# A cross-attention and FFN kernel: tiles of 128 queries, scores on row strips, fp32 products, and a written order for each engine

## What is computed

```python
q = (x @ Wq).reshape(b, n, 32, 8); k, v = split(ctx @ Wkv)       # x: layernormed
q, k = apply_axial_rope(q, pos), apply_axial_rope(k, pos)
w = softmax(einsum('bqhd,bkhd->bhqk', q, k) / sqrt(8))
x = x + einsum('bhqk,bkhd->bqhd', w, v).reshape(b, n, 256) @ Wout + bout
h = square(relu(ln(x) @ up_w))                                     # 256 -> 1024
y = h @ down_w + (ln(x) @ expert_weight) * top2(ln(x) @ gate_w).sum()
x = x + layernorm(y) * gamma + beta
```

## Time and profile before

| | us |
|---|---|
| median of 3 runs | 252.93 |
| lowest and highest | 249.64, 253.37 |
| span of the profiled execution | 250.5 |

### The profile page before, as it was taken

One profiled execution on the slowest core, in us unless ns is written; L12 is line 12 of the kernel. 1 busy time (PEld: TensorE's weight loads), 2 busy tenths in 40 slices (PEclk: granted clock), 3 DMA queues, 4 the chain that ended last, 5 costly groups with the idle time before them and its releaser, 6 DMA issues.

```text
span 250.5 us, 4919 instructions
## 1 busy us (share of the span) xinstructions
PE 221.1 (88%) x1754; PEld 175.5 (70%) x1754; DVE 167.7 (67%) x374; ACT 141.3 (56%) x284; POOL 105.3 (42%) x129
## 2 busy tenths in 40 slices
PE   2959768899999999999998999998889999778980
PEld 1847535677777787879786878877557886567980
DVE  6965899868886789684559974745998100572455
ACT  3256457597767675865647667564446967111520
POOL 7774566731238014474653136231324454332003
PEclk9995799999999999999999999999999999955896
DMA  7943141102101101010101110101000000000001
GB/s 199 357 94 84 47 107 45 28 20 62 48 24 29 42 3 48 0 48 0 47 0 43 46 47 0 46 3 44 0 27 21 5 0 3 0 0 22 3 21 42
DMA packets 12743, 10.68 MB, mean 43 GB/s; under 512 B 2992, under 2 KB 12336, under 8 KB 12720
## 3 DMA queue, kind: packets, MB, share of 16 engines
q1 hardware_dynamic: 11680, 10.37, 14.7%
q10 hardware_dynamic: 1040, 0.01, 0.2%
HBM read 5.13 MB, written 1.05 MB: 25 GB/s over the span
## 4 chain that ended last, share of the span: by engine, by line
PE 68%; DVE 18%; issue 6%; ACT 3%; POOL 2%; DMA 1%; POOLq 0%; DVEq 0%; ACTq 0%
PE ps_bg L956 18%; PE ps_bg L939 11%; PE ps_st L1037 11%; PE ps_o L1053 10%; PE ps_s L1021 9%; PE ps_dn L1109 9%; DVE mneg L837 7%; DVE stats L702 2%; DVE mnat L844 1%; PE ps_st L972 1%; DMA pos_sb<-in_fside_BxSx 1%; DVE mnat L845 1%; DVE by_token L710 1%; ACT kmask L612 1%; DVE rot_c L766 1%
## 5 line engine op out<-in xcount | busy, mean ns | idle before, releaser
L837 DVE TENSOR_REDUCE mneg<-ps_s 128x2 f32<-128x512 f32 x128 | 84.6, 684 | 36.4 <-PE ps_s L1021 35.7
L641 ACT ACTIVATE probs<-ps_st 128x512 f32<-128x512 f32 x128 | 73.3, 595 | 26.4 <-PE ps_st L1037 26.1
L1037 PE MATMUL ps_st<-qstack,kmask 128*128 128x256 f32 x256 | 57.3, 308 | 0.5 <-ACT probs L641 0.4
L1021 PE MATMUL ps_s<-kmask,qstack 128*128 128x512 f32 x128 | 54.4, 428 | 3.1 <-DVE mneg L837 1.9
L1037 PEld LDWEIGHTS ps_st<-qstack,kmask 128*128 128x128 f32 x256 | 39.9, 189 | 15.1 <-issue 9.5
L473 POOL TENSOR_SCALAR var_eps<-mv 128x1 f32<-128x1 f32 (+1 forms) x20 | 7.1, 353 | 75.0 <-DVE mv L705 74.9
L1053 PE MATMUL ps_o<-probs,vaug 128*32 128x256 f32 x512 | 34.3, 385 | 0.0
L1021 PEld LDWEIGHTS ps_s<-kmask,qstack 128*128 128x128 f32 x128 | 25.1, 197 | 7.2 <-DVE mneg L837 5.2
L956 PE MATMUL ps_bg<-x2nT,up 128*128 128x256 f32 x192 | 27.3, 296 | 1.0 <-ACT x2nT L573 1.0
L956 PEld LDWEIGHTS ps_bg<-x2nT,up 128*128 128x128 f32 x192 | 26.1, 202 | 2.0 <-ACT moe L672 1.4
L1109 PE MATMUL ps_dn<-down,inner 128*128 128x256 f32 x192 | 25.4, 283 | 0.2 <-DVE inner L341 0.2
(11 more groups left out here) (109 smaller groups left out, 311.5 us busy)
## 6 DMA issues: line engine op xcount, KB each, us to landing
kmask<-kstack SPq DMA_DIRECT2D x60, 64.0 KB, 2.1
x_sb<-in_x SPq DMA_DIRECT2D x4, 256.0 KB, 6.6
whole<-in_L_ffn_down_w SPq DMA_DIRECT2D x4, 256.0 KB, 5.4
qstack<-mT SPq DMA_DIRECT2D x64, 4.0 KB
result<-y_fin SPq DMA_DIRECT2D x8, 128.0 KB, 1.7
c_sb<-in_ctx SPq DMA_DIRECT2D x4, 128.0 KB, 2.4
oT<-in_L_ffn_up_w SPq DMA_DIRECT2D x1, 512.0 KB, 5.5
y_fin<-in_L_ffn_up_w SPq DMA_DIRECT2D x1, 512.0 KB, 7.4
```

Of the source, the lines that this page charges most:

```text
L641: act.activation(probs[n % 2][:, i, :, :], ps_st[k % NST][:].rearrange("p (t n) -> p t n", t=T), ACT.Exp, scale=SCALE).then_inc(st_free, 1)
L837: dve.tensor_reduce(mneg[m % 2][:, t, n % 2, 2 * half:2 * half + 2], ps_s[(4 * n + k) % NS][:].rearrange("p (i k) -> p i k", i=2), AX.X, A ...
L1021: pe.matmul(ps_s[(4 * n + k) % NS][:], qstack[b % 2][:, g, t * P:(t + 1) * P], kmask[:, g, 2 * half:2 * half + 2, :], start=True, stop=Tru ...
L1037: ins = pe.matmul(ps_st[k % NST][:, t * N:(t + 1) * N], kmask[:, g, i, t * P:(t + 1) * P], qstack[b % 2][:, g, :], start=True, stop=True)
```

## The change

The kernel is rewritten around another tiling; what is computed stays the same.

- Five written orders (`PE_ORDER`, `DVE_ORDER`, `ACT_ORDER`, `POOL_ORDER`, `SP_ORDER`) replace the one list with due times. An entry is a kind and its numbers.
- The tile is 128 queries (8 tiles `u`); a step `M` (32 of them) is one tile and one pair of head groups, 8 heads. FFN, output and expert products go by tile `u`.
- S and ST are matmuls on one row strip of 32 rows, so `kmask` and its DMAs go. An entry `B.k.n` of `PE_ORDER` is a burst: the two ST units number `k-1` on two strips and the two S units number `n-1` on the other two, interleaved.
- K and Q are computed transposed (weights as the loaded operand, their columns permuted by ScalarE at the start), so the 128 transposes of `nat` go. cos and sin are spread over rows and transposed once per batch (`TR`). Six DMAs for K and six for each part of Q (`shi`, `slo`) put the high and low parts into the rows of `kstack` and `qstack`.
- All products with weights are plain fp32, without split.
- The maxima are split on GpSimd (`mh`), most normalisations and squares are there too.
- PSUM: three banks for S, three for ST, two for all else, now with P·V and down. Four `probs` buffers. No `keep_warm`.

```diff
+PE_ORDER = """
+cT.0 V.0 TR.0 K.0 xT.0.0 cT.1 xT.0.1 Q.0.0 TR.1 TR.2 Q.0.1 xT.1.0 TR.3 K.1 V.1 cT.2 B.0.1 Q.1.0 B.0.2 xT.2.0
+B.0.3 K.2 MT.0 B.0.4 B.0.5 B.0.6 MT.1 B.1.7 Q.2.0 xT.3.0 B.2.8 MT.2 B.3.9 PV.0 B.4.10 MT.3 B.5.11 PV.1 MT.4
+B.6.12 B.7.13 PV.2 MT.5 B.8.14 B.9.15 PV.3 MT.6 B.10.16 o.0 B.11.17 PV.4 MT.7 B.12.18 aT.0 B.13.19 W.0 MT.8
...
+B.60.0 up0.3 B.61.0 E.3 x2T.5 up1.4 dna.2 dna.3 dnb.2
+dnb.3 E.4 up1.5 E.5 up0.4 PV.26 PV.27 PV.28 B.62.0 PV.29 B.63.0 PV.30 B.64.0 up0.5 PV.31 o.6 o.7 aT.6 aT.7 W.6
+W.7 dna.4 dna.5 dnb.4 dnb.5 x2T.6 x2T.7 E.6 up1.6 E.7 up0.6 up1.7 up0.7 dna.6 dna.7 dnb.6 dnb.7
...
+SP_ORDER = """
+ldc.0 ldwkv ldx.0.0 ldx.0.1 ldwq ldc.1 ldx.1.0 ldwout ldexpert ldup lddown ldc.2 ldx.2.0 ldc.3 ldx.3.0 ldvec
+shi.k.0 slo.k.0 slo.q.0.0 shi.q.0.0 shi.q.0.1 slo.q.0.1 shi.k.1 slo.k.1 shi.q.1.0 sM.0 slo.q.1.0 sM.1 sM.2 sM.3
+sM.4 sM.5 sM.6 sM.7 sM.8 sM.9 shi.k.2 shi.q.2.0 sM.10 slo.k.2 slo.q.2.0 sM.11 sM.12 sM.13 sM.14 sM.15 sM.16
...
-    LAG = 4
-    HB = 2
-    NS, NST = 2, 2
+    NS, NST, NBG = 3, 3, 2
+    MROW = Q - 2
+    NPROBS, NNEG = 4, 3
...
+                    w, b, n = e[1], e[2], cols(e)
+                    to = (kstack if w == "k" else qstack)[b % 2]
+                    source, ready = (hi[w], hi_ready) if what == "shi" else (lo[w], lo_ready)
+                    copies = {("shi", "k"): (0, 1), ("slo", "k"): (2,), ("shi", "q"): (0, 2), ("slo", "q"): (1,)}[what, w]
...
+                        sp.wait_ge(st_free, HG * T * NM * (b - 1))
+                    for c in copies:
+                        for half in range(2):
+                            rows = to[2 * c + half::8, :, n]
+                            sp.dma_start(rows.bitcast(f32), source[:, half, n].bitcast(f32)).then_inc(done, 16)
...
+                elif what == "mh":
+                    M = e[1]
+                    pool.wait_ge(s_free, max(S_NO[M, i] for i in range(HG)) + 1)
...
+                    link(pool.tensor_scalar(high.bitcast(f32r), of, 1.0, 0.0, ALU.mult, ALU.add))
+                    pool.tensor_tensor(low.bitcast(f32r), of, high, ALU.subtract).then_inc(mnat_ready, 1)
...
+            def product(to, lhs, rhs):
+                for k in range(len(lhs)):
+                    ins = pe.matmul(to, lhs[k], rhs[k], start=(k == 0), stop=(k == len(lhs) - 1))
                 return ins
...
+            def plain(M, i, s):
+
+                b, t, m = place(M)
+                rows = slice(Q * i, Q * i + MROW)
+                return pe.matmul(ps_s[S_NO[M, i] % NS][:, s * N:(s + 1) * N], qstack[b % 2][rows, 2 * m + s, tile(t)],
+                                 kstack[b % 2][rows, 2 * m + s, :], start=(s == 0), stop=(s == 1))
...
+            def transposed(M, i, s, k):
+                b, t, m = place(M)
+                at = (s * T + k) * P
+                return pe.matmul(ps_st[ST_NO[M, i] % NST][:, at:at + P], kstack[b % 2][strip(i), 2 * m + s, tile(k)],
+                                 qstack[b % 2][strip(i), 2 * m + s, tile(t)], start=(s == 0 and k == 0),
+                                 stop=(s == 1 and k == 1))
...
+                if what == "B":
+                    units = burst_units(e)
+                    for s in range(2):
+                        for k in range(2):
+                            for kind, M, i in units:
+                                if kind == "ST":
+                                    if s == 0 and k == 0:
+                                        transposed_wait(M, i)
+                                    ins = transposed(M, i, s, k)
...
+                                elif k == 0:
+                                    if s == 0:
+                                        plain_wait(M, i)
+                                    ins = plain(M, i, s)
...
+                    for f in range(4):
+                        ins = product(bg(e)[:, tile(f)], [up[:, k, tile(4 * j + f)] for k in range(KC)],
+                                      [x2nT[u % 2][:, k, :] for k in range(KC)])
```

More of the change, by code:

```diff
@@ L105, in xattn_ffn_kernel, with items @@
+sM.28 sM.29 out.1 sM.30 sM.31 out.2 out.3 out.4 out.5 out.6 out.7
+"""
+S_PHASE = 1
+def items(text):
+    return [tuple(int(w) if w.isdigit() else w for w in item.split(".")) for item in text.split()]
 def xattn_ffn_kernel(nc, x, ctx_in, pos, Wq, Wkv, Wout, bout, gate_w, up_w, down_w, expert_w,
@@ L119, in xattn_ffn_kernel @@
     HG = 4
-    G = H // HG
+    NM = 4
+    G = 2 * NM
     Q = P // HG
@@ new lines, in xattn_ffn_kernel, with burst_units @@
+    bursts = {}
+    for e in pe_order:
+        if str(e[0])[0] == "B":
+            bursts[e] = len(bursts)
+    def burst_units(e):
+        units = []
+        if e[1]:
+            k = e[1] - 1
+            units += [("ST", k // 2, 2 * (k % 2) + r) for r in range(2)]
+        if e[2]:
+            k = e[2] - 1
+            h = (k + S_PHASE) % 2
+            units += [("S", k // 2, 2 * h + r) for r in range(2)]
+        return units
+    in_strips = [u for e in pe_order if e[0] == "B" for u in burst_units(e)]
@@ new lines, in xattn_ffn_kernel @@
+        mneg = [sb(f"mneg{i}", [P, HG, 2]) for i in range(NNEG)]
+        mnat = [sb(f"mnat{i}", [P, 2, HG * 2]) for i in range(2)]
+        mT = [sb(f"mT{i}", [2 * HG * 2, P], f32r) for i in range(2)]
+        probs = [sb(f"probs{i}", [P, HG, 2, T, P]) for i in range(NPROBS)]
+        oT = [sb(f"oT{i}", [P, NM, P]) for i in range(2)]
+        rden = sb("rden", [P, 2, 4 * HD])
+        attn = [sb(f"attn{i}", [P, D]) for i in range(2)]
+        attnT = [sb(f"attnT{i}", [P, KC, P]) for i in range(2)]
@@ L242, in xattn_ffn_kernel @@
+        x2n = [sb(f"x2n{i}", [P, D]) for i in range(2)]
+        x2nT = [sb(f"x2nT{i}", [P, KC, P]) for i in range(2)]
+        top8 = sb("top8", [P, U, 8])
+        route = sb("route", [P, U])
+        moe = [sb(f"moe{i}", [P, D]) for i in range(2)]
+        whole = [sb(f"whole{i}", [P, 4, P]) for i in range(2)]
+        inner = [sb(f"inner{i}", [P, FT, P]) for i in range(2)]
+        y = [sb(f"y{i}", [P, D]) for i in range(2)]
+        fin = [sb(f"fin{i}", [P, D]) for i in range(2)]
         ps_s = [bank(f"ps_s{i}") for i in range(NS)]
@@ L357, in xattn_ffn_kernel @@
-        PIECES += [(whole[j % HB][:], lambda i, j=j: down[:, i, 2 * j:2 * j + 2, :],
-                    (ld_down[j % HB], 16 * (j // HB + 1)), down_split) for j in range(FT // 2)]
-        PIECES += [(raw_expert, lambda i: expert[:, i, :, :], (ld_expert, 32), weights_split)]
-        piece_slots = [int(slot) for slot in PIECE_SLOTS.values()]
-        assert len(set(piece_slots)) == len(PIECES) and piece_slots == sorted(piece_slots)
-        later_loads = [(piece_slots[UPS - 1] + 2, "expert", weights_split, UPS)]
@@ L365, in xattn_ffn_kernel, with strip, place @@
[L365 to L371 removed]
+            eng.wait_ge(bg_free[TURN[e] % NBG], TURN[e] // NBG + 1)
+        def strip(i):
+            return slice(Q * i, Q * (i + 1))
+        def place(M):
+            return M // (T * NM), M // NM % T, M % NM
@@ L452, in _ @@
+            for i in range(2):
+                sp.wait_ge(out_done[i], 16 * U // 2)
         @block.gpsimd
```

1398 lines of the change are left out of this document (598 added, 800 removed), and 14 rows, old and new, of tables (AFTER, AFTER_1, BESIDE_LAST, LAST).

## The result

The changed kernel takes **233.5 us** (median of 4 runs, 232.15 to 237.54) where the kernel before takes 253.15 beside it (249.64 to 253.68): a ratio of 0.924, 95% interval 0.916 to 0.932. The forecast was 238.5 with a range of 217 to 265. The profiled execution took 237.54, with a span of 235.7 us.

What follows compares the result with a forecast made beforehand. TensorE's instruction steps were taken to bound the kernel: start 35 + middle 161.9 + end 39.4 = 236.3 us of span, plus 2.4 to the median, 238.7, say 238.5. Own range 224 to 250; from D to A, 217 to 265.

Steps and rivals of the forecast that it cites:

- The mechanism: In the middle, TensorE sets the time and a burst's four row strips run side by side, 0.47 us a burst.
- rivals A: In the ST strips of every burst, 128-column f32r matmuls stream at fp32's rate: 26.5 us, time 265; chance 0.14.
- B: In the bursts, strips do not overlap and loads take turns: 58 us, time 297; chance 0.06.
- C: Two banks and three busy engines eat the gain: waits 20% instead of 8.9%, +16.5 us, time 255; chance 0.16.
- D: Bursts cheap and row switches nearly free: middle 20 us less, time 217; chance 0.12.
- Steps: TensorE's work at full clock: burst 0.47, switch 0.17, P·V round 0.115, fp32 instructions 0.118 or 0.23; sum 191.4 us.
- Waits: In the middle, 8.9% waits on 148.7 us of TensorE's work, giving 161.9 us.
- its own sign: The prediction falls if the clock falls in the middle stretch; no size was given.
- The start: Up to the first ST: keys split at 14 us, then 17.4 + 1.2 + 2.1, so 34.7, near 35 us.
- this costs nothing as long as six bursts fit: In the start, the first S moving from 19 to about 24 us is free if six bursts fit before 35.
- The end: After the last P·V: 27.7 us of work, 6.7 without a matmul, 5 for normalisation and colder clock: 39.4 us.
- Slack on the other engines: In the middle, VectorE about 100 us and ScalarE about 108 us; neither passes 70% of 160 us.

Runs made afterwards that it cites:

- the changed kernel again: Nothing altered: the changed kernel run and profiled once more beside three of the experiments; 234.13 us, ratio 0.925, profiled span 229.3 us.

## Why the prediction was right, and where it was not

The mechanism held in the middle. TensorE's instructions set most of it, the burst costs 0.44 where 0.47 was put, and rivals A (decides from 0.67) and B (1.52 with its switch, on one strip) are out by the trace and by a run. C put waits at 20%; the trace has 9.1 us on 139.2, 6.5%. D is out too: a switch costs 0.148 on average. The other parts of the change (fp32 instead of split products, K and Q transposed, five orders) were not undone one by one; what each is worth rests on the steps alone.

The total came out as near as it did partly by luck: the start was 5.7 us too short, and the middle and the end too long, so the misses cancelled in part.

- *Steps.* Nearly every price was a little high, the switch most: 0.17, taken from the one kind of change that the kernel before had in its rows, where the many kinds here average 0.148. 11.9 us too much in the sum, 9.5 of it in the middle.
- *Waits.* 8.9% were put on, 13.2 us. The trace has 9.1 us and up to 10.2 us of half clock. The clock in the middle stretch was named as what would make the prediction fall; it did fall, so by its own sign this term failed, and the cheaper steps covered it. 161.9 was forecast for the middle. 154.3 was measured in the changed kernel again, 7.6 less; the 160.7 of the slowest execution is near the forecast only because 20.4 us at half clock made up for the steps, which is luck.
- *The start.* 35 was forecast, 40.7 measured. Two terms failed: "the first keys are split at about 14 us" (they are split at 18.3 and their spread is issued at 18.4, behind a copy held up for 3.4 us), and 28 issues at 0.62, which took 20 us with their waits instead of 17.4; from there to the first ST it is 2.3 us where 3.3 were put. The idea that this costs nothing as long as six bursts fit was wrong in another way: TensorE stood waiting there and its clock fell. The prediction also counted the idle transposes that go as 3.7 us gained and put nothing for the clock of the start; with idle work in its waits the kernel is 3 us faster.
- *The end.* 39.4 was forecast, 34.3 measured. The work is 26.2 us at the measured steps, 5.4 us stand behind the last matmul (6.7 before), and only 2.7 between them where 5 were put for normalisation and a colder clock.
- *Slack on the other engines.* Right for VectorE, by the run with half the maxima. But the run with 20.7 us less of TensorE's work gave back 8.4: the margin to the next limit is small, above all in the end, which the prediction didn't ask.
- *The own range.* From 238.5, +9 for the waits gives 247.5; the "250" is not what the terms add up to. Nothing hangs on it.

Net against the forecast: start +5.7, middle -7.6, end -5.1 in the changed kernel again, a span of 229.3 where the sum had 236.3; in the slowest execution the middle is -1.2 and the span 235.7.

## What to carry to other kernels

Price a TensorE schedule by the step from one instruction to the next at full clock, with a price for every change of mode, and then ask separately what the clock will be: in the profiles of the changed kernel 13 and 24 us stand at half clock, some 6 to 12 us of time, where all changes of mode make 23. Where TensorE must wait for a start-up chain, idle work in its waits can be worth more than shortening the chain: here the first gave 3 us, and the second, alone, nothing. Removing work from the busiest engine pays only up to the next chain: a run that leaves work out tells how far that is.

## What the runs showed of the hardware

- Four row strips with different shapes (128 and 256 columns) run side by side in both orders of issue that were tried: 0.592 and 0.602 us a burst, against 1.52 on one strip.
- A switch between row strips, column strips and the whole array costs 0.148 us on average, and 0.17 beside fp32 instructions with 256 columns.
- VectorE's copy of 16 columns took 3.44 us while GpSimd was filling buffers, 0.18 without that. The Trainium skill, "SBUF — State Buffer", section "Who interferes with whom", says that a copy in VectorE's two-port mode and a GpSimd instruction exclude each other, and that the one that comes second waits; the trace agrees as far as it shows (the copy's mode stands in no row), and here the copy ended only at 7.09 us, behind a whole row of memsets (the last ends at 7.05), not behind one.
- The granted clock stood at half in the start of every kernel: for 10.2 to 23.9 us in all between 17 and 52 us without idle work in the waits there, for 3.4 us with it. Idle work in another place did not do it: the kernel before had 30 idle transposes ahead of 15 us and stood at half from 17.9 to 24.8 and from 28.2 to 31.6 us.
- In the middle a wait alone does not decide: one of 1.86 us at 117 us was followed by no fall, one of 1.24 at 121 us was. And with all units on one strip the clock fell at 182.8 us after 17.8 us in which TensorE was busy throughout. What decides stays open.
